# A three-block decoder layer on one core: a reordered opening with a DRAM path for the first queries, and the causal mask of the first score pass moved from TensorE into VectorE's maxima

## The reference, cut to what matters

```python
q = (x @ Wq.T).reshape(b, s, NH, HD).transpose(0, 2, 1, 3)   # NH = 16 heads, HD = 8
k = ...; v = ...
q = _apply_rotary(q, cos, sin); k = _apply_rotary(k, cos, sin)
attn = jnp.einsum('bhqd,bhkd->bhqk', q, k) * scale
attn = jnp.where(causal, -jnp.inf, attn)      # causal = triu(ones, k=1)
attn = jax.nn.softmax(attn, axis=-1)
out = jnp.einsum('bhqk,bhkd->bhqd', attn, v)
...
x = x + _L0_attn_ref(_layernorm(x), ...)
x = x + _L0_xattn_ref(_layernorm(x), ctx_1024, ...)   # same, no mask, keys from ctx
x = x + _L0_ffn_ref(_layernorm(x), ...)               # 2 of 8 experts for each sequence
```

## Time and profile before

| | us |
|---|---|
| median of 3 runs | 212.4 |
| lowest and highest run | 211.24, 214.91 |
| the profiled execution, its own time | 211.94 |
| its span, first to last instruction | 210.2 |
| PE busy in the span | 181.0 |
| DVE busy | 139.0 |
| ACT busy | 104.4 |
| POOL busy | 51.7 |

### The profile page before, as it was taken

One profiled execution on the slowest core, in us unless ns is written; L12 is line 12 of the kernel. 1 busy time (PEld: TensorE's weight loads), 2 busy tenths in 40 slices (PEclk: granted clock), 3 DMA queues, 4 the chain that ended last, 5 costly groups with the idle time before them and its releaser, 6 DMA issues.

```text
span 210.2 us, 4262 instructions
## 1 busy us (share of the span) xinstructions
PE 181.0 (86%) x1552; PEld 115.6 (55%) x1552; DVE 139.0 (66%) x337; ACT 104.4 (50%) x222; POOL 51.7 (25%) x101
## 2 busy tenths in 40 slices
PE   0749389838999999999999899899999999799994
PEld 0413367625555656654655554364565455398994
DVE  3799478832456678779889888979887527524220
ACT  2130023313456465556466576666866575695441
POOL 4460028895000042011011003001106107107040
PEclk9999979995699999999999999999999999999999
DMA  5815431474504301340340340210070070070630
GB/s 147 226 49 151 140 102 50 138 177 120 134 2 127 102 2 56 101 115 9 100 122 5 92 134 5 72 44 2 5 227 5 2 225 5 4 221 25 173 107 25
DMA packets 25292, 18.64 MB, mean 89 GB/s; under 512 B 2424, under 2 KB 23416, under 8 KB 24696
## 3 DMA queue, kind: packets, MB, share of 16 engines
q1 hardware_dynamic: 24048, 17.79, 30.5%
q10 hardware_dynamic: 1224, 0.59, 1.0%
HBM read 11.36 MB, written 2.10 MB: 64 GB/s over the span
## 4 chain that ended last, share of the span: by engine, by line
PE 64%; DVE 19%; DMA 7%; issue 2%; ACTq 2%; POOL 2%; ACT 2%; SPq 1%; POOLq 0%; DVEq 0%
PE psV L872 12%; PE psA L824 11%; PE psB L851 10%; PE psV L934 6%; DVE negmax L592 5%; DMA stackQ<-maxT 4%; PE psA L917 4%; PE psM L882 3%; PE psB L856 3%; PE psA L829 3%; PE psM L754 3%; DVE stats L528 2%; PE psM L892 2%; ACTq L680 2%; DMA stackQ<-hid 2%
## 5 line engine op out<-in xcount | busy, mean ns | idle before, releaser
L708 ACT ACTIVATE E<-psB 128x512 f32<-128x512 f32 x112 | 62.6, 597 | 53.9 <-PE psB L856 32.0
L592 DVE TENSOR_REDUCE negmax<-psA 128x2 f32<-128x512 f32 (+1 forms) x112 | 72.6, 682 | 21.0 <-PE psA L829 19.0
L824 PE MATMUL psA<-stackK,stackQ 72*128 72x256 bf16 (+1 forms) x256 | 44.8, 268 | 8.5 <-DVE negmax L592 4.5
L851 PE MATMUL psB<-stackQ,stackK 74*128 74x256 bf16 (+1 forms) x256 | 42.3, 266 | 4.6 <-DMA stackQ<-maxT 4.5
L872 PE MATMUL psV<-E,V 128*9 128x256 f32 (+1 forms) x512 | 36.6, 358 | 0.0
L824 PEld LDWEIGHTS psA<-stackK,stackQ 72*128 72x128 bf16 x256 | 21.2, 101 | 25.2 <-DVE negmax L592 12.8
L851 PEld LDWEIGHTS psB<-stackQ,stackK 74*128 74x128 bf16 x256 | 23.9, 100 | 11.2 <-DMA stackQ<-maxT 5.2
L447 POOL TENSOR_SCALAR rstd<-mv 128x2 f32<-128x2 f32 x12 | 2.8, 235 | 107.7 <-DVE mv L532 107.6
L934 PE MATMUL psV<-w2s,hid 128*128 128x128 f32 x128 | 16.4, 277 | 0.8 <-ACT hid L735 0.8
L934 PEld LDWEIGHTS psV<-w2s,hid 128*128 128x128 f32 x128 | 15.7, 192 | 1.5 <-issue 1.2
L829 PE MATMUL psA<-mask,ident 128*128 128x256 bf16 (+1 forms) x48 | 15.9, 332 | 0.0
(11 more groups left out here) (111 smaller groups left out, 218.8 us busy)
## 6 DMA issues: line engine op xcount, KB each, us to landing
stackK<-scratch SPq DMA_DIRECT2D x18, 192.0 KB
stackQ<-hid SPq DMA_DIRECT2D x45, 64.0 KB
w1s<-w_dram SPq DMA_DIRECT2D x8, 258.0 KB, 2.8
w2s<-w_dram SPq DMA_DIRECT2D x8, 256.0 KB, 4.1
stackK<-hid SPq DMA_DIRECT2D x18, 64.0 KB
stackQ<-scratch SPq DMA_DIRECT2D x2, 576.0 KB
scratch<-hid SPq DMA_DIRECT2D x4, 192.0 KB, 4.6
scratch<-parts_ctx SPq DMA_DIRECT2D x4, 192.0 KB, 2.2
```

Source lines behind the costliest of these rows:

```text
L592: dve.tensor_reduce(negmax[:, b, h:h + nh, t], psA[:, bank].rearrange("p (h k) -> p h k", h=nh), AX_X, ALU.max, negate=True).then_inc(a_ta ...
L708: act.activation(dst, psB[:, bank].rearrange("p (h q) -> p h q", h=dst.shape[1]), ACT.Exp, scale=SCALE).then_inc(b_taken, 1)
L824: last = pe.matmul(psA[:, bank, i * keys:(i + 1) * keys], stackQ[0:ROWS, b, h, t * P:(t + 1) * P], stackK[0:ROWS, b, h, 0:keys], start=(s ...
L851: last = pe.matmul(psB[:, bank, i * n:(i + 1) * n], stackK[:, b, h, t * P:(t + 1) * P], stackQ[:, b, h, q0:S], start=(s == 1 or i == 0), s ...
```

## The change

1. **Mask by VectorE.** In the first pass of self jobs PE's mask matmul is gone (it stays in the second pass). DVE takes each head by itself with `tensor_tensor_reduce`: it adds `row_mask` (fp32, zeros for the first 128 columns and the causal triangle for the last 128) to the scores, times -1, writes the result to a throwaway tile `masked` in bf16 and keeps the minimum as `negmax`. It also waits on its own `a_taken` for the unit two back.
2. **First queries through DRAM.** The nine ACT-issued fills of sequence 0's `stackQ` become two writes to `scratch` (parts 0 and 1, then part 2) and two reads back. Sequence 1's nine SP-issued fills become one write by ACT and one read by SP.
3. **Order.** POOL sets its constants between the first layer norms and not after all four. Two context turns, a K and a V projection of the cross side move into the opening, with 10 warming matmuls ahead of and 10 behind the projections, in place of 16. `ln_apply` of sequences 2 and 3 come later. The projections of sequences 2 and 3 go to the banks of `psB`, one half ahead of a new step `rope` that uses them. `max_rows` of job 0 stands directly behind its last unit, and the scratch write and read of sequence 2 come after it, those of sequence 3 further back.

```diff
-WARM = 16
+WARM = 10
+    start = [("ln_stats", 0, 0), ("constants", 0, 0), ("ln_apply", 0, 0), ("ln_turn", 0, 0), ("ln_stats", 0, 1),
+             ("constants", 0, 1), ("ln_apply", 0, 1), ("ln_stats", 0, 2), ("ln_stats", 0, 3), ("qk_self", 0, 0),
+             ("ln_turn", 0, 1), ("qk_cast", 0, 0), ("qk_self", 0, 1), ("stack_put", 0, 0), ("ctx_turn", 1, 0),
+             ("ctx_turn", 1, 1), ("keep_warm", 0, 0), ("stack_fill", 0, 0), ("stack_get", 0, 0), ("k_cross", 1, 0),
+             ("v_cross", 1, 0), ("keep_warm", 0, 1), ("stack_put", 0, 1), ("stack_fill", 0, 1), ("stack_get", 0, 1),
+             ("ln_apply", 0, 2)]
...
+    put(3, "rope", 0, 2)
+    put(7, "max_rows", 0, 0)
+    put(8, "rope", 0, 3)
+    put(9, "stack_write", 0, 2)
+    put(10, "stack_read", 0, 2)
+    put(14, "stack_write", 0, 3)
...
+                if kind == "stack_get" and b == 1:
+                    sp.wait_ge(scr_q_self[b], 16)
+                    read_q(s, b)
...
-                    dve.tensor_reduce(negmax[:, b, h:h + nh, t], psA[:, bank].rearrange("p (h k) -> p h k", h=nh),
-                                      AX_X, ALU.max, negate=True).then_inc(a_taken, 1)
+                    scores = psA[:, bank].rearrange("p (h k) -> p h k", h=nh)
+                    if s == 0:
+                        keys = (t + 1) * P
+                        if unit == 0:
+                            dve.wait_ge(row_mask_set, 1)
+                        if unit >= 2:
+                            dve.wait_ge(a_taken, unit - 1)
+                        for i in range(nh):
+                            last = dve.tensor_tensor_reduce(out=masked[:, bank, i * keys:(i + 1) * keys], in0=scores[:, i, 0:keys],
+                                                            in1=row_mask[:, S - keys:S], scale=-1.0, scalar=LARGEST,
+                                                            op0=ALU.add, op1=ALU.min,
+                                                            accum_out=negmax[:, b, h + i, t:t + 1])
+                        last.then_inc(a_taken, 1)
+                        continue
...
+                if kind == "stack_put" and b == 0:
+                    act.wait_ge(parts_q_self[b], 2)
+                    act.dma_start(scratch[0, b, 0, 0:2].rearrange("i p t -> p i t"),
+                                  parts[:, b, 0, 0:2]).then_inc(scr_q_self[b], 16)
+                    act.wait_ge(parts_q_self[b], NPART)
+                    act.dma_start(scratch[0, b, 0, 2], parts[:, b, 0, 2]).then_inc(scr_q_rest, 16)
+                if kind == "stack_get" and b == 0:
+                    act.wait_ge(scr_q_self[b], 16)
+                    act.dma_start(stackQ[0:2 * BLOCK, b], thrice(0, b, 0, 2)).then_inc(q_in[b], 16)
+                    act.wait_ge(scr_q_rest, 16)
+                    act.dma_start(stackQ[2 * BLOCK:ROWS, b], thrice(0, b, 2, 1)).then_inc(q_in[b], 16)
...
-                    if s == 0:
-                        blocks = psA[:, bank].rearrange("p (h k) -> p h k", h=len(heads))[:, :, keys - P:keys]
-                        last = pe.matmul(blocks, ident16[:, :], mask16[:, 0:len(heads), :], start=False, stop=True,
-                                         skip_group_check=True)
```

More of the change, by code:

```diff
@@ L160, in plan @@
         misc = []
-        first_qk = kind == "qk_self" and b < 2
-        for _ in range(0 if first_qk else uses.get(kind, 0)):
+        for _ in range(uses.get(kind, 0)):
             bank = total % 2
@@ L260, in build, with own_q, own_k @@
         psM = ctx.enter_context(nc.psum_tensor("psM", [P, 2, 512], F32))
+        def own_q(b):
+            return 32 if b == 0 else 16
+        def own_k(b):
+            return 16 * NFILL if b < 2 else 16 * NPART
         def up_bank(q):
@@ L297, in build, with thrice @@
         dve_own, pool_own = sem("dve_own"), sem("pool_own")
+        def thrice(s, b, i, n):
+            src = scratch[s, b, 0, i:i + n]
+            return bass.AP(src.tensor, src.offset, [[NH * S, n * HD], [0, NPART], [1, NH * S]])
         block = ctx.enter_context(nc.Block())
@@ L355, in _ @@
                             fill_k(b, i, r, parts_k_self[b])
-                if kind == "stack_fill" and (s == 1 or b > 0):
+                if kind == "stack_fill" and s == 1:
                     for i in range(NPART):
                         for r in range(NPART):
-                            fill_q(b, i, r, parts_q[b] if s == 1 else parts_q_self[b])
+                            fill_q(b, i, r, parts_q[b])
+                if kind == "stack_get" and b == 1:
+                    sp.wait_ge(scr_q_self[b], 16)
+                    read_q(s, b)
                 if kind == "stack_write" and s == 0:
@@ L442, in _ @@
             pool.memset(ones[:, :], 1.0).then_inc(consts, 1)
+            pool.memset(euler[:, :], 2.718281828459045).then_inc(consts, 1)
+            pool.memset(ident16[:, :], 0.0)
+            then(pool.memset(row_mask[:, :], 0.0))
+            then(pool.memset(mask16[:, :, :], 0.0))
             def rsqrt_var(n, b):
@@ L454, in _ @@
                     rsqrt_var(st["norm"], b)
-                if kind == "constants":
-                    constants()
-                if kind == "qk_self" and b >= 2:
-                    for bank, k in misc:
-                        pool.wait_ge(misc_taken[bank], k)
+                if kind == "constants" and b == 0:
+                    pool.affine_select(out=ident16[:, :], in_=ident16[:, :], compare_op=ALU.not_equal, fill=1.0, base=0,
+                                       pattern=[[-1, P]], channel_multiplier=1).then_inc(consts, 1)
+                    causal(mask16, 1)
+                    pool.wait_ge(consts, 4)
+                    pool.tensor_copy(row_mask[:, P:S], mask16[:, 0, :]).then_inc(row_mask_set, 1)
+                if kind == "constants" and b == 1:
+                    then(pool.memset(mask16T[:, :, :], 0.0))
+                    causal(mask16T, -1)
+                if kind == "rope":
+                    pool.wait_ge(rope_first, b + 1)
                     for w, ready in ((1, parts_k_self[b]), (0, parts_q_self[b])):
@@ L675, in _ @@
                             act.activation(parts[:, b, w, n], rot[:, b, 0, w], ACT.Copy).then_inc(ready, 1)
-                if kind == "stack_fill" and s == 0 and b == 0:
-                    for i in range(NPART):
-                        for r in range(NPART):
-                            act.wait_ge(parts_q_self[b], i + 1)
-                            act.dma_start(stackQ[i * BLOCK + r:(i + 1) * BLOCK:NPART, b],
-                                          parts[:, b, 0, i]).then_inc(q_in[b], 16)
+                if kind == "stack_put" and b == 0:
[4 more added lines that the diff above has]
+                    act.dma_start(scratch[0, b, 0, 2], parts[:, b, 0, 2]).then_inc(scr_q_rest, 16)
+                if kind == "stack_put" and b == 1:
+                    act.wait_ge(parts_q_self[b], NPART)
+                    act.dma_start(scratch[0, b, 0].rearrange("i p t -> p i t"),
+                                  parts[:, b, 0]).then_inc(scr_q_self[b], 16)
+                if kind == "stack_get" and b == 0:
[3 more added lines that the diff above has]
+                    act.dma_start(stackQ[2 * BLOCK:ROWS, b], thrice(0, b, 2, 1)).then_inc(q_in[b], 16)
                 if kind == "ctx_turn":
@@ L771, in _ @@
                     taken("ln_turn", 0, b)
-                    dst, full = (psB[:, b], qk_full) if b < 2 else (psM[:, bank], misc_full[bank])
+                    if b >= 2:
+                        pe.wait_ge(rope_first, b - 1)
                     for w in range(2):
-                        last = pe.matmul(dst[:, w * S:(w + 1) * S], wQK[:, w, :], xnT[:, b, :], start=True, stop=True)
-                    last.then_inc(full, 1)
+                        last = pe.matmul(psB[:, b % 2, w * S:(w + 1) * S], wQK[:, w, :], xnT[:, b, :], start=True,
+                                         stop=True)
+                    last.then_inc(qk_full, 1)
                 if kind == "v_self":
@@ L849, in _ @@
                         pe.wait_ge(ones_in, 32)
+                        pe.wait_ge(consts, 5)
+                    if unit < 2:
+                        pe.wait_ge(rope_first, unit + 3)
                     for i, h in enumerate(heads):
```

94 lines of the change are left out of this document (38 added, 56 removed).

## The result

The changed kernel takes 204.34 us in the median of four runs (203.86 to 207.05), the kernel before 212.19 (211.24 to 214.91). The ratio is 0.965, with a 95% interval of 0.961 to 0.969: 3.5% faster. I had forecast no change that can be told, 211.3 us within 206 to 221. The profiled execution took 203.86 us, against 211.94. Some executions of a kernel take a few per cent longer, at a lower granted clock, and the ratios leave these out.

A forecast was written before the change was run, and what follows sets the result against it. PE bounds the overlapped stage, DVE and the maxima's DMA the time before. First score 22.3 + 25.4 = 47.7, + 43.7 = 91.4 against 92.0, hence 211.94 - 0.6 = 211.3 us, range 206 to 221.

The forecast's parts named there:

- The cost of a head: DVE's self-job maxima: 0.21 or 0.35 us a head plus 0.11 for its second instruction, 3.1 us a group against 2.0.
- The sum around it: Stage times: 25.4 us from first score to first exponential at 47.7, then 43.7 to the last self maximum at 91.4.
- by a hair: From first exponential to last self maximum, DVE at 40.0 us narrowly becomes the bound over PE at 39.1.
- PE's 39.1: PE's need from first exponential to last self maximum: 43.7 less 10 x 0.46 us, slow clock included.
- What leaves PE: Mask matmuls gone from the first pass: 0.46 us a group, 7.4 in 16 groups, worth nothing in the first stretch.
- The opening: Time up to the first score: 22.3 us instead of 24.0, bounds 20.8 and 24.5.
- (b): In the opening, ACT's two writes and two reads replace nine query fills; first write lands about 16.5 us, reads take 4.5 to 5.5.
- The K fills are unchanged: In the opening, SP's fills of K go on beside the queries' new DRAM reads and stay as they were.
- The stall goes, and DVE's work takes its place.: Ahead of the first exponential: the 6.08 us maxima DMA wait vanishes, but DVE work keeps it at 47.7 us, from 48.2.
- cheap reads: Rival: a group costs DVE 2.9 us, first score at 20.8, PE bounds again; 206 us, chance 0.17.
- rival 2: Each DVE head instruction waits for the one ahead, a group costs 4.1 us; 224 us, chance 0.15 with all groups from 3.5.
- rival 3: PE idles through a DVE-bound first stage and stays at 1.2 GHz for 16 us, not 9; 216 us, chance 0.12.

The follow-up runs named there:

- Late max_rows: Changed kernel with max_rows of job 0 one half later and sequence 2's scratch write and read put back ahead of it on SP; 210.7 us, ratio 0.998.
- serial heads: Changed kernel where DVE waits after each head of a unit, except the last, for that head's second instruction; 211.7 us, ratio 1.001.
- both masks: Changed kernel with PE's mask matmuls put back in the first pass while DVE keeps adding the mask by heads; 207.6 us, ratio 0.979.
- direct fills: Changed kernel with sequence 0's queries filled as before, by nine ACT-issued DMAs from SBUF without the DRAM path; 209.6 us, ratio 0.990.
- K of 1 late: Changed kernel where SP holds back sequence 1's nine K fills until both stacks of sequence 0 have landed; 206.4 us, ratio 0.979.
- warm longer: Changed kernel with 32 warming matmuls in place of 10 in the second group; 204.9 us, ratio 0.965.
- no mask: Changed kernel with no mask in the first pass, one tensor_reduce over each unit's unmasked scores; 204.7 us, ratio 0.963.

## Why the prediction was wrong, point by point

- **What bounds the kernel.** Right: PE in the overlapped stage, DVE and the maxima's DMA ahead of it, PE at half clock behind that wait. Late max_rows reproduced the last two together.
- **The cost of a head: the step that failed.** "I take 0.11, nearer to the lower end", for the second instruction. It costs nothing: it starts with the next head's operation. The two other numbers, 0.21 and 0.35, were right to 0.01 us. I had bounded the read by what an instruction of its own takes and so never gave "below what any row shows" a place; the bound "no time at all" had a reason, since the next head needs nothing from it. With eight reads in a group this put 0.9 us too much into each of 16 groups: 14 of the 18 us that I added, where DVE's busy time rose by 4.0.
- **The sum around it** holds up to the first exponential. With 2.2 for a group and the first score at 24.0, the prediction's own lines give 24.0 + 5 x 2.2 + 0.84 + 5.3 + 3.3 = 44.4 for the first exponential (45.1 measured). Behind it DVE needs 10.7 x 2.2 + 6.9 + 3.7 = 34.1 us, less than PE's 39.1: PE is the bound and not DVE, and the last self maximum comes at 83.5 (82.9 measured). That is the balance tipping the other way, which "by a hair" should have warned of. The serial heads put 0.6 of the 0.9 us back into each group and gave 211.7 us, close to my forecast. That 83.5 is so near is in part luck, as the next point shows.
- **PE's 39.1** had the second stretch's half clock in it. The clock was full there: 8.8 us at 0.53 are 4.7 at full clock, and 4.7 + 34.9 - 4.6 = 35.0. The stage took 37.8. The two gains, full clock and no mask matmuls, did not come in full, and the end point of the stage was off too: I took 92 for the last self maximum, which is at 90.4. With the mask matmuls and no half clock (both masks) the stretch to the marker takes 41.2 us, against 43.4 before and 38.8 after. The full clock, with all else in which both masks differs from the kernel before, is then worth 2.2 us there and the matmuls 2.5, not 4.1 and 4.6.
- **What leaves PE**: 0.46 us a group, 4.6 in the overlapped stage. Both masks against after shows 2.5 there, and 1.0 in the first stage, where I had put nothing.
- **The opening.** Wrong in size: 24.0 and not 22.3. POOL's masks did get out of DVE's way (two operations of 256 elements take 0.76 us, and took 1.21). (b)'s first write left ACT at 13.82, near the 13.65 that I had, and landed at 15.85, 2.0 us later; I had named 2.5 and summed with 2.2. But Q's last read was there at 23.17 and not 22.3, and "The K fills are unchanged" failed: their last landed 2.4 us later than before, beside Q's reads, and behind Q. I had looked at the queries' path because the chain named it, and not asked what its new traffic does to the fills beside it. PE stood idle for 5.4 us ahead of the first score, where I had some 3.
- **"The stall goes, and DVE's work takes its place."** The stall went, as said. DVE's work took its place only in part, for the price above.
- **The rivals.** The first one, cheap reads, had 0.17 and 206 us; it needed the opening's gain as well and still priced the read at 0.085. None of them let it fall to nothing. Its own terms also give 211.3 - 1.5 - 3 - 1.5 = 205.3, not 206, which was the lower end of my range. Serial execution (rival 2) did not come. The Trainium skill, page "VectorE: DVE Perf Modes", section "Two Vector instructions with no wait between them", says that an instruction is held only by a change of start quadrant, and the trace agrees: the next head starts 0.21 us after one that lasts 0.29. The half clock of rival 3 did come, for 17.7 of the 21.1 us of the first stage, but ended 0.6 us behind the first exponential, so the dear part of rival 3 did not.

## What to carry to other kernels

A short instruction whose result the next one doesn't need may be free, so bound its cost from nothing up, and read starts rather than durations. Where two engines are within a few per cent of each other, the forecast is decided by the least known price of either: give the case in which that price vanishes its full weight. An 8 KB transfer on the way to the next stage goes into the queue ahead of the large ones that are wanted later; in this kernel that move was worth 1.3% in the old order and 3% in the new, part of it probably through TensorE's clock behind the wait. And a new path for one transfer is to be charged for what it does to those beside it: here it made Q earlier and K later.

## What the runs showed of the hardware that I had not expected

- DVE's `DVE_READ_ACCUMULATOR2_ANT` lasts 0.08 us and starts with the next operation, so it adds nothing to the start-to-start time (0.21 us on 128 elements, 0.34 on 256). A semaphore wait between two such heads adds 0.12 us each.
- 10 us more of DVE work cost 7.4 us of time. 3 us less gained nothing by itself (204.7 us), and 2 us together with more warming matmuls (202.2 us).
- Nine fills of 64 KB from SBUF to eight rows of a stack: the last lands 3.5 us after its issue in the kernel before and 3.75 in direct fills, where nine such fills of Q run beside them, but 6.01 in the changed kernel, where reads of 0.6 MB from DRAM do, and 6.64 in K of 1 late, without nine more fills behind them in the same queue.
- Where the half clock outlasts the first exponential, the stretch from there to the marker is longer: 38.8 us with 0.6 us of it (after), 39.5 with 3.7 (warm longer), 40.2 with 6.6 (no mask).
